# A fused transformer block with routed experts: when GpSimd takes the later inverse roots, and how result gathers and weight-row loads share the tail

## The reference, cut to what matters

```python
x = x + ga * _L0_attn_ref(h, L0_attn_inter_palace_weight)
h = _layernorm(x, axis=-1) * (1 + cb) + sb
# _L0_ffn_ref(h): xt is h as (n, 128)
shared = relu(xt @ sW1 + sb1) @ sW2 + sb2
probs = softmax(xt @ router_W + router_b)
top_p, top_i = top_k(probs, 3)                 # cw: weight of each expert, 0 if not chosen
h = relu(einsum('nd,edh->neh', xt, eW1) + eb1)
ye = einsum('neh,ehd->ned', h, eW2) + eb2
x = x + gb * (shared + einsum('ned,ne->nd', ye, cw))
```

## Time and profile before

| | |
|---|---|
| median of 3 runs | 377.3 us (375.74 to 377.87) |
| the profiled execution's own time | 377.16 us |
| its span | 375.6 us |
| granted TensorE clock, mean | 0.961 |
| PE busy | 321.9 us (86%) |
| ACT busy | 286.2 us (76%) |
| DVE busy | 164.9 us (44%) |
| POOL busy | 82.7 us (22%) |

### The profile page before, as it was taken

The page is one execution under the profiler, slowest core; times in us unless marked ns, Lnnn a source line. Parts: engine busy times, 40 slices in busy tenths (PEclk is TensorE's granted clock), DMA queues, the critical chain, the costliest instruction groups (busy, mean ns, idle before and its releaser), DMA issues.

```text
span 375.6 us, 6507 instructions
## 1 busy us (share of the span) xinstructions
PE 321.9 (86%) x2355; PEld 146.2 (39%) x2355; DVE 164.9 (44%) x508; ACT 286.2 (76%) x284; POOL 82.7 (22%) x105
## 2 busy tenths in 40 slices
PE   4879799998999999899998999997599299999822
PEld 2632222222333223233222223321478296767521
DVE  7993014235152372442622303500265079877942
ACT  3679889999999999999999999997165265443311
POOL 4891001601000000100000656700010000067730
PEclk9999989999999999999999999999699699999985
DMA  7788899151000799700000011124844897912211
GB/s 219 253 316 293 276 364 307 48 188 66 3 2 0 268 308 391 241 0 2 3 0 2 29 38 49 51 80 125 268 113 117 249 384 230 384 39 77 83 31 61
DMA packets 37908, 55.94 MB, mean 149 GB/s; under 512 B 3888, under 2 KB 20818, under 8 KB 37232
## 3 DMA queue, kind: packets, MB, share of 16 engines
q1 hardware_dynamic: 35900, 51.92, 41.3%
q0 software_dynamic: 1536, 3.16, 3.0%
q10 hardware_dynamic: 436, 0.39, 0.3%
HBM read 34.92 MB, written 22.51 MB: 153 GB/s over the span
## 4 chain that ended last, share of the span: by engine, by line
issue 28%; PE 18%; POOL 13%; SPq 11%; DMA 11%; DVE 9%; ACT 8%; ACTq 1%; POOLq 0%; DVEq 0%
PE acc L1653 8%; ACT prob L840 7%; POOL xs_d L767 6%; SPq L574 5%; PE slot L1558 4%; SPq L575 4%; POOL QQ L778 4%; DMA val<-cw_d 3%; DMA xs_d<-xtok,line 2%; POOL val L778 2%; DMA cw_d<-cwT 2%; DMA KK<-kw 1%; PE slot L1713 1%; POOL rstd L689 1%; DMA kw<-w1l 1%
## 5 line engine op out<-in xcount | busy, mean ns | idle before, releaser
L840 ACT ACTIVATE prob<-slot 128x1536 f32<-128x1536 f32 x171 | 233.5, 1489 | 8.8 <-PE slot L1558 8.3
L1653 PE MATMUL acc<-prob,val 128*18 128x512 f32 x1024 | 136.4, 605 | 2.7 <-DVE oT L1145 1.8
L1558 PE MATMUL slot<-QQ,KK 32*128 32x512 f32 (+1 forms) x768 | 92.9, 410 | 11.6 <-ACT prob L840 8.2
L1558 PEld LDWEIGHTS slot<-QQ,KK 32*128 32x128 f32 x768 | 43.9, 187 | 130.0 <-ACT prob L840 93.9
L689 POOL TENSOR_TENSOR rstd<-rstd,power 128x4 f32<-128x4 f32 (+1 forms) x6 | 7.4, 1241 | 198.9 <-DVE rstd L984 198.9
L869 ACT ACTIVATE ghi<-prob 128x512 fp32r<-128x512 f32 x26 | 16.4, 632 | 31.5 <-DVE prob L1383 31.5
L1653 PEld LDWEIGHTS acc<-prob,val 128*18 128x18 f32 x1024 | 17.4, 96 | 31.9 <-issue 28.9
L778 POOL DMA_INDIRECT QQ<-ys_d,line x16 | 16.0, 1001 | 58.8 <-DMA val<-cw_d 54.2
L767 POOL DMA_INDIRECT xs_d<-xtok,line x24 | 23.9, 996 | 7.3 <-issue 6.4
L1145 DVE COPY oT<-acc 128x512 f32<-128x512 f32 x8 | 5.5, 692 | 42.9 <-PE acc L1653 42.9
L896 ACT ACTIVATE prob<-slot,rows 128x128 f32<-128x128 f32 x38 | 10.9, 373 | 11.0 <-DMA ys_d<-prob 6.5
(11 more groups left out here) (282 smaller groups left out, 359.9 us busy)
## 6 DMA issues: line engine op xcount, KB each, us to landing
KK<-wcat SPq DMA_DIRECT2D x32, 128.0 KB, 2.0
KK<-kd SPq DMA_DIRECT2D x14, 256.0 KB, 5.6
QQ<-qd SPq DMA_DIRECT2D x14, 256.0 KB, 6.0
KK<-kw SPq DMA_DIRECT2D x14, 256.0 KB, 6.4
KK<-cw_d SPq DMA_DIRECT2D x3, 1024.0 KB, 7.5
xs_d<-ffT SPq DMA_DIRECT2D x1, 2580.0 KB, 14.6
rows<-xs_d SPq DMA_DIRECT2D x10, 258.0 KB, 4.1
ys_d<-prob SPq DMA_DIRECT2D x10, 256.0 KB, 5.3
```

The costliest lines, as they stand in the source:

```text
L840: nc.scalar.activation(ring[:, at:at + n * CH], slot[u % 2][:, 0:n * CH], ACT.Exp, scale=SCALE).then_inc(exp_done, 1)
L1558: return mm(dst, KK[n][r, s, c * M:(c + 1) * M], QQ[n][r, lo:hi], start=True, stop=True, tile_position=(32 * q, 0))
L1653: last = mm(acc[32 * q:32 * q + 2 * HV], val[:, b, n // 2, c, q, HV * odd:HV * odd + 2 * HV], prob[:, (G * cl + q) % RING], start=c == 0 a ...
```

## The change

GpSimd's order becomes: roots of stages 0 and 1, the scatters, roots of stages 2 and 3. The gathers of stage 0 no longer wait for chunks 4 to 7 of the row loads; those of stage 1 do. SyncE issues chunks 4 to 7 only when the gathers of stage 0 have landed. VectorE takes the results of stage 0 in job 16 (sum in job 22), and those of stage 1 behind the last job.

```diff
@@ SyncE
             routing(1)
+            sp.wait_ge(gath[0], 16 * QC * K)
             for k in range(CHUNKS, DENSE * CHUNKS):
                 row_chunk(k)
@@ GpSimd
-            for _ in range(LAST):
+            for _ in range(SORTED):
                 root_guess(0, QC)
...
-            root_guess(0, QC)
+            for _ in range(SORTED, STAGES):
+                root_guess(0, QC)
             for k in range(YRING):
                 pool.wait_ge(y_wr[k], 16 * len(range(k, GROUPS, YRING)))
-            for k in range(DENSE * CHUNKS):
-                pool.wait_ge(rows_ld[k], 16 * len(row_buffers(k)))
             pool.wait_ge(pv_done, CLASSES)
             for s in range(SORTED):
+                for k in range(CHUNKS * s, CHUNKS * (s + 1)):
+                    pool.wait_ge(rows_ld[k], 16 * len(row_buffers(k)))
                 for k in range(K):
                     for i in range(QC * s, QC * (s + 1)):
                         p.indirect_dma_start(yacc[s][k][:, i % QC], None, ys_d, line_of(i, k)).then_inc(gath[s], 16)
@@ VectorE
-                if g == EXPERTS + 8:
+                if g == EXPERTS:
                     three_results(0)
-                if g == EXPERTS + 9:
+                if g == EXPERTS + 6:
                     stage_sum(0)
-                if g == EXPERTS + 14:
-                    three_results(1)
+            three_results(1)
             stage_sum(1)
```

## The result

The changed kernel takes **357.23 us** (median of 4 runs, 356.41 to 357.3) against 376.86 us before (4 runs on the same occasion, 375.74 to 377.87): a ratio of 0.9475, interval 0.9443 to 0.9507. Forecast were 360.2, with a range of 355.5 to 368. The profiled execution took 356.41 us, with a span of 354.7. So the change pays 5.3% here. On the two later occasions on which this kernel was run again it paid far less, though; that is what most of the experiments are about.

A forecast was written before the change was run, and what follows sets the result against it. Three things were taken to end the time: scatters begun late, a full SyncE queue, gathers begun late ahead of the last job. Jobs starting 13.9 us earlier plus 3.1 net behind gave 17.0, from 377.16 to 360.2 us; range 355.5 to 368.

The forecast's parts named there:

- Part 1: GpSimd's scatters, put ahead of the root of stage 2, run from 187.90 and land at 225.05, 21 us earlier.
- Part 2: The root of stage 2 now waits for the scatters; its late rows cost 1.1 us, bounds 0 and 1.1.
- Part 3: SyncE's loads start at 225.05 and end at 270.7; both TensorE gaps close, 13.1 us; last scaled result at 296.4.
- The clock: Without gaps TensorE's clock should not fall: 0 to 3.8 us saved, 1.9 taken.
- Part 4: Tail: twelve gathers, chunks 4 to 7, then twelve more; dense jobs lose 5 us, net gain behind the jobs' start 3.1.
- The rule against it: Busy VectorE beside stage 0's gathers may starve GpSimd's DMAs; forecast too early by some microseconds, without a figure.
- Rival A: Gathers stretched and stores landing late: 7.6 us at the most, 367.8; half of it 364; chance 0.11.
- The end: From the first final add to the span's end 6.6 us, giving a span of 358.6 us.
- B: Slower weight loads beside attention leave TensorE's 7.14 us gap before group 7: 367.3, with cold clock 368.3; chance 0.08.
- C: The head does nothing, the scatters being held by something not seen: 374.0 us; chance 0.04.
- D: The root of stage 2 becomes the bound if scatters slow; 19 us more needed to end over 379.2; chance 0.04.

The follow-up runs named there:

- e1: The kernel before with only the new order of root and scatters: 384.27 us, ratio 1.0105; repeated on the third occasion 378.56 us, ratio 0.9945.
- e2: The changed kernel with the old order of root and scatters, keeping the tail's turns: 377.17 us, ratio 0.9926.
- e3: The changed kernel without SyncE's wait for the gathers of stage 0: 384.40 us; repeated on later occasions 374.50 and 379.50 us.
- e4: The changed kernel with chunk 4 issued ahead of SyncE's wait: 369.15 us, ratio 0.9731; repeated on the fourth occasion 375.12 us, ratio 0.9814.
- e0_again: The changed kernel, instruction for instruction, with one blank line added, on the second occasion: 378.08 us, ratio 0.9944 to the kernel before.

## Why the prediction was right, and where its sizes were off

The forecast of 360.2 was 3.0 us above the median and 3.8 above the profiled execution. That it came so close is in part luck: its two largest errors, 4.9 and 2.9 us, go against each other. The gain in the profiled spans was 20.9 us, where 17.0 were forecast. Up to the last scaled result it was 18.8 in place of 13.9; from there to the first final add it was 0.2 in place of 3.1; and 1.9 came behind that add, where nothing was expected. By its steps, against that trace:

- **Part 1, the scatters**, right: 187.9 to 225.05 was the forecast; in the trace GpSimd's copy starts at 185.40 and SyncE goes on at 222.41. The length agrees (37.15 and 37.0 us); the start is 2.5 earlier. That is no effect of the change: nothing ahead of it was edited, and in ten later profiles of kernels with this order GpSimd's copy starts anywhere from 185.41 to 189.44. A sum made against one execution carries such a term unseen.
- **Part 2, the waiting root**, over-sized: 1.1 was taken, TensorE waited 0.20 us, and ScalarE not at all.
- **Part 3, SyncE and the gaps**, right: the weights end at 269.1 (forecast 270.7, or 268.2 with the early start), and both gaps are gone. The clock was under-sized: the stretch from the first tile rows to the last scaled result was 310.29 - 267.24 - 7.14 = 35.9 us before and is 291.51 - 258.80 = 32.7 now, so 3.2 us and not 1.9. The last scaled result came at 291.51 for 296.4: 2.5 by the start, 0.9 by the root, 1.3 by the clock, 0.2 left over.
- **Part 4, the stores and gathers**, right in order, but the 3.1 us that it credits to taking turns are not there. The last store landed after 6.61 us (5.3 taken, 7.8 allowed), the first block took 14.81 us (14.2), gate 17 ran 4.6 behind its landing as forecast, and the second block took 15.22 (14.2). Each is small; together they eat the whole gain of the tail: 349.98 - 291.51 = 58.5 us from the last scaled result to the first final add, against 369.00 - 310.29 = 58.7 before and 352.0 - 296.4 = 55.6 in the forecast.
- **The rule against it** has the direction right and no more. The 24 gathers were 25.5 us busy (16.4 and 9.1 in the page's groups) against 23.7 before: 1.8 us more, with single ones at 1.25 to 1.31 us, while VectorE was busy for 82% of the two blocks against 71% before. In direction that agrees with what the Trainium skill, SBUF — State Buffer, says in the box on "DVE blocks DMA"; in which mode VectorE's operations ran, no trace here shows, and later profiles have the 24 gathers anywhere from 23.0 to 25.3 us. Rival A had allowed 7.6 for it, and left the later landing of the stores, which it names (2.5 us), out of its 367.8.
- **The end**, wrong by 1.9: from the first final add (349.98) to the span's end lie 4.7 us, where 6.6 were carried over from before. SyncE's two last stores took 1.16 us to issue instead of 1.85; why is not known. All twelve later profiles have 6.1 to 7.7 us there, so this 1.9 is most likely no effect of the change.

Rivals B and C did not happen. D, the root as the bound, did not in the form it had: no scatter took longer. But it is near what the later occasions show, that scatters beside attention cost attention time. The prediction looked for that price in GpSimd's own durations and in the landing, and there it does not stand.

What nothing in the prediction allowed for is that **the saving rests on the other engines running on undisturbed while GpSimd issues its DMAs**. Where they do, the change gives 5.3%, and by the profiles nearly all of it in the head. Where they do not, the cushion is gone and 0.6 to 1.5% remain, on the edge of what can be told: the same kernel took 378.08 and 377.23 us there, outside the range of 355.5 to 368. That the forecast held is thus also luck of the occasion.

What is open: the second and third occasion were on one chip, the fourth on another, and both showed the standstills; whether the first ran on a better chip or in a better hour can't be told, and the parts (e1, e2, e3, e4) were never run where the changed kernel takes 357 us. How the gain divides between head and tail there is only argued, from two profiled executions: 18.8 us are there at the last scaled result (310.29 less 291.51), 2.5 of them by the start, which the change does not touch. What makes an engine stand still while GpSimd issues a DMA was not found. Nor is it shown that e4_chunk4 beats the changed kernel on a calm occasion; on the third it did by 2.1% (369.15 to 377.23), and on the fourth it had the lowest ratio of the complete kernels, with no run of the changed kernel beside it.

## What to carry to other kernels

A stage that starts late only because its producer stands behind an unrelated step of the same engine is worth moving, and the sum can be read from the old trace: the length of the stage, the next full queue, and the gap that this queue had hidden. When a wait is placed between bulk loads, leave ahead of it the one load that the next gate needs. And before counting a gap as pure loss, ask what it hides on another chip or day: run the changed kernel on several occasions, and look in the other engines for standstills while GpSimd issues indirect DMAs.

## What the runs showed that was not expected

- One program took 356.4 to 357.3 us on one occasion and 371.8 to 380.6 on two others; the kernel before 375.7 to 377.9 against 378.1 to 388.6. A ratio measured on one occasion (0.9475) did not hold on others (0.9944, 0.9853).
- There, a row of eight scatters 1.26 us apart goes in most rounds with a standstill of ScalarE of 1.7 to 4.1 us near its end, and 24 gathers in a row with waits of up to 12.8, of which 5.6 with the input ready. GpSimd's own durations do not show it: the scatters take 0.96 us in both, and the gathers of e3_nowait are even quicker (0.94 at most times) than those of the changed kernel on the first occasion, of which several took 1.25.
- Each standstill of 3 us goes with more loss than itself; the likely reason is that TensorE's granted clock falls behind it (0.56 in the 4 us after the first in e0_again). ScalarE's three standstills of 8.5 us together came with 6.2 us of waiting for TensorE's scores in between, 0.4 on the first occasion, and the first tile rows were 15.4 us late.
- Taking turns in the tail brought next to nothing on the calm occasion (0.2 us between two profiles) and 5 to 8 us in the profiles of the disturbed ones, where the unbroken row of gathers costs most. Which of two changes pays can depend on the occasion.
